# A new instruction order in the second phase of a fused LayerNorm, linear-attention and MLP kernel

## The reference

```python
def reference(x, ...):
    y = layernorm(x)
    h = layernorm(y) * g1 + b1
    q, k, v = h @ wq, h @ wk, h @ wv          # 16 heads of 16
    phi_q, phi_k = elu(q) + 1, elu(k) + 1
    kv, z = sum_s(phi_k * v), sum_s(phi_k)    # per sequence and head
    y2 = y + ((phi_q @ kv) / (phi_q @ z + 1e-6)) @ wo
    h = layernorm(y2) * g2 + b2
    g = table[clip(round((h @ w1) / 0.1))]    # gelu on a grid, 1024 wide
    x = x + y2 + g @ w2
    return x + (layernorm(x) @ CB.T) * (SCB / 127) + bias
```

## Time and profile before

| what | value |
|---|---|
| median of 3 runs | 651.34 us (648.35 to 652.54) |
| time of the profiled execution | 651.4 us |
| its span, first to last instruction | 649.6 us |
| mean granted TensorE clock | 0.975 of full speed |

### The profile page before, as it was taken

One profiled execution on the slowest core, in us unless ns is written; L12 is line 12 of the kernel. 1 busy time (PEld: TensorE's weight loads), 2 busy tenths in 40 slices (PEclk: granted clock), 3 DMA queues, 4 the chain that ended last, 5 costly groups with the idle time before them and its releaser, 6 DMA issues.

```text
span 649.6 us, 12205 instructions
## 1 busy us (share of the span) xinstructions
PE 586.2 (90%) x3838; PEld 517.6 (80%) x3838; DVE 517.0 (80%) x1076; ACT 411.7 (63%) x767; POOL 386.2 (59%) x337
## 2 busy tenths in 40 slices
PE   6999999999997999898998989989899898998875
PEld 6887787878786878788787978879788797887675
DVE  5488988898873688878888788887988878888656
ACT  2377767676765685675756757576665766657560
POOL 3446475655542447676486765757657576675553
PEclk8599999999997999999999999999999999999898
DMA  8101112021101000000100001010110000100001
GB/s 287 53 34 65 59 38 65 32 65 34 66 1 36 17 32 33 32 32 32 65 32 32 33 33 65 32 32 32 32 65 32 32 32 32 65 24 11 33 1 67
DMA packets 11128, 29.16 MB, mean 45 GB/s; under 512 B 2016, under 2 KB 4576, under 8 KB 11104
## 3 DMA queue, kind: packets, MB, share of 16 engines
q1 hardware_dynamic: 9472, 28.32, 12.3%
q10 hardware_dynamic: 1632, 0.53, 0.4%
HBM read 20.45 MB, written 8.39 MB: 44 GB/s over the span
## 4 chain that ended last, share of the span: by engine, by line
PE 36%; DVE 27%; issue 16%; POOL 12%; ACT 6%; DMA 1%; DVEq 1%; ACTq 0%; POOLq 0%; SPq 0%
PE psum L914 31%; DVE f_arena L729 8%; POOL f_arena L355 5%; DVE bn_stats L615 5%; PE psum L932 4%; POOL rstd L324 3%; DVE f_arena L755 3%; DVE f_arena L657 2%; DVE mean_var L622 2%; ACT grid_index L540 2%; DVE f32r_arena L738 2%; POOL pow_arg L322 2%; ACT f32r_arena L550 2%; ACT f32r_arena L494 1%; DVE f_arena L642 1%
## 5 line engine op out<-in xcount | busy, mean ns | idle before, releaser
L914 PE MATMUL psum<-w_hi,f32r_arena 128*128 128x256 f32 x1280 | 178.7, 286 | 5.1 <-DVE f32r_arena L738 3.5
L914 PEld LDWEIGHTS psum<-w_hi,f32r_arena 128*128 128x128 f32 x1280 | 164.9, 190 | 16.0 <-issue 11.5
L914 PE MATMUL psum<-f32r_arena,w_hi 128*128 128x512 f32 x512 | 143.0, 411 | 3.7 <-issue 3.7
L540 ACT ACTIVATE grid_index<-psum,w_bias_in_steps 128x512 int8<-128x512 f32 x128 | 87.2, 681 | 69.9 <-PE psum L914 69.9
L729 DVE TENSOR_SCALAR f_arena<-f_arena,mean_var,rstd 128x256 f32<-128x256 f32 x124 | 102.7, 887 | 25.9 <-POOL rstd L324 25.9
L914 PE MATMUL psum<-f32r_arena 128*128 128x512 f32 (+1 forms) x512 | 120.5, 378 | 2.6 <-issue 1.5
L343 POOL TENSOR_TENSOR f32r_arena<-f_arena,f32r_arena 128x512 fp32r<-128x512 f32 x64 | 86.0, 1344 | 56.3 <-ACT f32r_arena L550 56.3
L914 PEld LDWEIGHTS psum<-f32r_arena,w_hi 128*128 128x128 f32 x512 | 91.1, 194 | 22.4 <-ACT grid_index L540 4.7
L932 PE MATMUL psum<-ident,f_arena 128*128 128x128 f32 x504 | 69.6, 283 | 36.9 <-DVE f_arena L729 32.3
L932 PEld LDWEIGHTS psum<-ident,f_arena 128*128 128x128 f32 x504 | 58.6, 145 | 52.1 <-issue 28.3
L914 PEld LDWEIGHTS psum<-f32r_arena 128*128 128x128 f32 x512 | 83.2, 190 | 14.9 <-issue 3.1
(11 more groups left out here) (96 smaller groups left out, 976.4 us busy)
## 6 DMA issues: line engine op xcount, KB each, us to landing
f_arena<-in_L_attn_x_dram SPq DMA_DIRECT2D x32, 512.0 KB, 3.3
out_dram<-f_arena SPq DMA_DIRECT2D x15, 512.0 KB, 2.6
f_arena<-in_L_attn_w_dram SPq DMA_DIRECT2D x2, 1024.0 KB, 11.3
out_dram<-f_arena SPq DMA_DIRECT2D x2, 256.0 KB, 2.2
phi_q<-in_L_attn_wk_dram ACTq DMA_DIRECT2D x1, 256.0 KB, 4.9
phi_q<-in_L_attn_wv_dram ACTq DMA_DIRECT2D x1, 256.0 KB, 5.4
phi_q<-in_L_attn_wq_dram SPq DMA_DIRECT2D x1, 256.0 KB, 5.7
phi_q<-in_L_ffn_CB_dram SPq DMA_DIRECT2D x1, 256.0 KB, 7.8
```

The source lines that it names most:

```text
L540: act(k8[:, m % 2], bank(AB + m % 2), ACT.Identity, scale=1.0 / STEP, bias=h_bias[:, m:m + 1]).then_inc(s["grid_ready"], 1)
L914: return nc.tensor.matmul(out_, lhs, rhs, start=start, stop=stop, skip_group_check=True)
```

## The change

Phase 2 is put in another order on four engines, and the second norm gets a buffer of its own (`n2t`) instead of sharing `nt`. No operation is added or removed.

```diff
 GpSimd, body
+                if main:
+                    wait(g, s["xp_ready"], i)
+                    g.wait_ge(s["y2_ready"], i + 1)
+                    nc.gpsimd.tensor_tensor(xz, x2[p], y2, ALU.add).then_inc(s["xz_ready"], 1)
                     mlp_low(i, 0)
                 if prv:
                     power(i - 1, u3, r3, mv3, "mv3_ready", "u3_ready", "pow3")
                 if main:
-                    wait(g, s["xp_ready"], i)
-                    g.wait_ge(s["y2_ready"], i + 1)
-                    nc.gpsimd.tensor_tensor(xz, x2[p], y2, ALU.add).then_inc(s["xz_ready"], 1)
                     mlp_low(i, 2)
+                if main:
+                    mlp_low(i, 4)
                 if nxt:
                     power(i + 1, u2, r2, mv2, "mv2_ready", "u2_ready", "pow2")
                 if main:
-                    mlp_low(i, 4)
+                    mlp_low(i, 6)
                 if nn:
                     first_norm(i + 2, p, turn + 1)
-                if main:
-                    mlp_low(i, 6)
 ScalarE, body
                 if main:
-                    quantise(i, 4)
+                    mlp(i, 4)
+                    quantise(i, 5)
                 if prv:
                     a.wait_ge(s["o_done"], o_before_c)
                     high(i - 1, "n3_turned", SA, "s_hi_c")
                 if main:
-                    gelu(i, 4)
-                    mlp(i, 5)
+                    gelu(i, 5)
                     mlp(i, 6)
+                    quantise(i, 7)
                 if nxt:
                     high_h(i + 1)
                 if main:
-                    mlp(i, 7)
+                    gelu(i, 7)
 VectorE, buffers and body
-        take(CE)
+        n2t = take(CE)
...
-            def normalise(c, src, mv, r, powered, done):
+            def normalise(c, src, dst, mv, r, powered, done):
...
-                normalise(c, y2, mv2, r2, "pow2", "n2_ready")
+                normalise(c, y2, n2t, mv2, r2, "pow2", "n2_ready")
...
                 if nxt:
                     first_residual(i + 1)
+                    norm2(i + 1)
                 if prv:
                     low(i - 1, SA, "s_hi_c", "s_lo_c")
-                if nxt:
-                    norm2(i + 1)
+                if main:
+                    mlp_low(i, 5)
                 if prv:
...
                     ve.tensor_tensor(tm(ot), two(SA).rearrange("p (j d) -> p j d", j=TT),
-                if main:
-                    mlp_low(i, 5)
+                if nn:
+                    attend(i + 2, 0)
                 if nxt:
                     low_h(i + 1)
-                if nn:
-                    attend(i + 2, 0)
                 if main:
                     mlp_low(i, 7)
 TensorE, body
                     if main:
                         down(i, 1)
                         up(i, 4)
+                        down(i, 2)
+                        up(i, 5)
                     if prv:
...
                         turn(nt, SA, "n3_turned")
                     if main:
-                        down(i, 2)
-                        up(i, 5)
                         down(i, 3)
                         up(i, 6)
+                        down(i, 4)
                     if prv:
...
                         rows(SA, s_hi, s_lo, cbh, cbl, not exact).then_inc(s["cb_done"], 1)
-                    if nxt and prv:
+                    up(i, 7)
+                    if attend_seq is not None:
+                        attention(i + 2, attend_seq, 0)
+                    if nxt:
                         turn2(i + 1)
-                        up(i, 7)
-                        down(i, 4)
-                        if attend_seq is not None:
-                            attention(i + 2, attend_seq, 0)
                     down(i, 5)
```

More of the change, by code:

```diff
@@ L723, in attend @@
                                      ALU.mult).then_inc(s["attn_tile"], 1)
-            def normalise(c, src, mv, r, powered, done):
+            def normalise(c, src, dst, mv, r, powered, done):
                 v.wait_ge(s[powered], c + 1)
                 for j in range(TT):
-                    i = ve.tensor_scalar(tm(nt)[:, j], tm(src)[:, j], mv[:, 2 * j:2 * j + 1], r[:, j:j + 1],
+                    i = ve.tensor_scalar(tm(dst)[:, j], tm(src)[:, j], mv[:, 2 * j:2 * j + 1], r[:, j:j + 1],
                                          ALU.subtract, ALU.mult)
@@ L789, in body @@
                     v.wait_ge(s["mv3_ready"], i)
-                    normalise(i - 1, xp, mv3, r3, "pow3", "n3_ready")
+                    normalise(i - 1, xp, nt, mv3, r3, "pow3", "n3_ready")
                 if main:
@@ L1096, in turn2 @@
                 pe.wait_ge(s["y2_ready"], c + 1)
-                turn(nt, of_chunk(c, SB2, AB), "n2_turned")
+                turn(n2t, of_chunk(c, SB2, AB), "n2_turned")
             def phase2(exact):
```

## The result

The changed kernel takes 674.26 us (median of 4 runs, 673.53 to 676.41) against 650.99 for the one before in the same comparison: a ratio of 1.037, 95% interval 1.033 to 1.041. It was forecast at 673, slower. The span of the profiled execution is 671.8 us, 22.2 more.

What follows compares the result with a forecast made beforehand. Phase 2's 13 equal bodies were taken as bounding, TensorE near its floor plus waits, with VectorE blocked while GpSimd works. Each body +2.0 us, +26 in all, ends -4.3: 651.4 becomes 673.1 us, range 658 to 690.

Steps and rivals of the forecast that it cites:

- step 1: GpSimd's `xz` ahead of block 0: block 0 and `down(0)` later, cost 0.65 us; first norm done about 10.3, not 12.0.
- T: Clock in us of the predicted walk through one body, starting at that body's `up(0)` on TensorE.
- the 0.65: Predicted cost in us per body of `down(0)` starting later because block 0 queues behind `xz` on GpSimd.
- step 2: n3 turned later on TensorE, behind `down(2)` and `up(5)`: reached at 13.1, norm done, gap of 1.6 us goes.
- step 3: Block 4 ahead of `pow2`, `norm2` ahead of CB's low part: CB starts at 19.0, new gap 2.1, net 0.9 lost.
- step 4: Attention and `turn2` behind `ot`: only `up(7)` covers VectorE's reading of CB; gap 0.5, `turn2` at 23.4.
- step 5: `gelu(7)` behind `high_h` at the body's end: block 7 late, GpSimd's output beside it; `down(7)` at 28.3, gap 1.2.
- the collision: GpSimd's output running beside VectorE's block 7 at the body's end: bounds 0 and 1.4 us, taken as 0.5.
- The sum of a body: Phase 2 body: 24.6 us of work plus gaps 0.2, 0.7, 2.1, 0.5, 1.2 make 29.3, against 27.3.
- The ends: Bodies outside the 13 equal ones: body 0 -0.3 us, body 14 -1.1, body 15 -2.9, together -4.3.
- The falling clock: Rival: granted clock also falls after the new gap at CB, +12 to +22 us, 685 to 695; chance 0.12.
- "It works as drawn": Rival: both TensorE gaps (1.6 + 0.7) go, no wait replaces them: 617 us in whole, 632 in half; chance 0.11.

Runs made afterwards that it cites:

- the two runs on the sum's place: Changed kernel with GpSimd's `xz` between block 0 and the third norm's power: 677.33 us; with `xz` back behind that power: 698.52 us.

## Why the prediction was right

**The sum first (step 1).** Block 0 ran T+4.0 to 5.3 and `down(0)` started at T+5.4, as walked. But the 0.65 can't be taken as a price: with block 0 in time CB started no earlier (T+18.9) and the kernel was slower. The step is right in the walk, and by the two runs on the sum's place the edit was a gain in this order.

**n3 (step 2).** Turned at T+13.0 without a wait (13.1 walked). The norm beside one block took 2.34 us and was done at T+10.0; about 3 us and 10.3 were walked.

**The norm ahead of the low part (step 3).** This is the cause, shown by the run that undoes it alone: 674.3 to 649.5, and 670.1 to 632.3 with GpSimd's output held in both. CB at T+18.8 (19.0 walked), gap 2.0 (2.1). The step's heading names two edits, and one half of it was wrongly accused: block 4 ahead of the power does hold the power, but without it block 4 holds the norm, and with the low part in front it gains 11 us.

**The wait for `ot` (step 4).** Half right. Where the clock stayed full, the attention waited 0.38 for `ot` (0.5 walked); where the clock fell and CB took 2.60 to 3.46, it waited 0 to 0.19. There `up(7)` took 1.33 to 1.91 in place of 1.10, and covered VectorE's reading of CB.

**The end (step 5).** `down(7)` waited 0.81 to 0.94 in bodies with the full clock and 0.47 in the others, walked as 1.2. The 0.5 that I took for the collision in every body was 0.4 in five of thirteen: this is the mis-sized term, and holding the output alone gained 4 us, not 6.5. It grew into the largest loss only in an order that I hadn't thought of.

**The sum of a body.** Walked 29.3, measured 29.05 where the clock stayed up and 29.7 where it fell, 29.45 on the mean. The forecast's body was 0.25 too long, its clock too good: two errors of 3 to 5 us that cancel in part, so the 673.1 against 674.3 is better than the working behind it. That is luck. The split of the sum is off too. By the view, TensorE idled 2.05 us in the body of the earlier trace rows (1.51, 0.47 and small ones), not 2.7, so its work is 25.2, not 24.6; in the changed kernel a body with the full clock has 25.4 of work and waits of 0.38, 1.97, 0.38 and 0.88, together 3.6 and not 4.7. The times of the walk on T don't hang on this split.

**The rivals.** The falling clock was given 0.12 and a price of 12 to 22 us, as another case. It was part of this one: it fell in 8 bodies, and filling the gap took 5 us out of the 13 bodies. I had placed the gap of 2.1 between one that left the clock alone and one that didn't; I should have put a part of the price into the sum. "It works as drawn" was named with the right condition, the low part done before TensorE gets to CB: met by one exchanged pair of lines, and with the collision removed it gave 632 against the 617 to 632 named.

**The ends.** Bodies 14 and 15: -1.5 and -3.2 against -1.1 and -2.9. Body 0 took 0.3 more, not 0.3 less. Together -4.4 against -4.3, which is closer than its parts; the start of phase 2, 1.1 us earlier, belongs to no step.

## What to carry to other kernels

In an order of instructions that wait on each other, ask of each instruction with a wait what stands behind it on its engine and who needs that. A step that is ready belongs ahead of one that waits, when another engine stands for it; the exchange of two such steps was worth 25 us here, and 38 with the collision behind it out of the way. When a gain fails to appear, look at the durations of unchanged instructions: a wait that keeps VectorE and GpSimd apart can be worth more than the time that it costs. And price a place in an order only together with what it hides: moving the sum from ahead of block 0 to behind it cost 3 us in one order and gained 6.5 in another. Last, compare the loop bodies and not the whole time alone, when a part that no edit touches differs by some us from trace to trace.

## What the runs showed of the hardware

VectorE's subtraction of two SBUF tiles (block 7) took 2.83 us in place of 0.69 when GpSimd's sum of 2.34 us started 0.06 us ahead of it. This is the exclusive lock on a port pair that the Trainium skill describes (SBUF — State Buffer, "Who interferes with whom"), here for an instruction with two SBUF inputs, and the trace agrees. What I hadn't expected is how cheaply it is avoided: put one behind the other by a wait, the same two instructions took 0.69 and 2.40 us.

The granted clock went to 1.2 GHz after TensorE's wait of 1.98 us, in 8 of 13 equal bodies, and not in the other five, with the same wait (1.97 in one of them). Before the change it stayed at 2.4 GHz through bodies with gaps of 1.5 and 0.5. The length of the wait alone doesn't tell: the clock fell in 9 bodies of 13 with a wait of 2.8 at CB (sum between block 0 and the power), in all 13 with one of 2.95 (sum behind the power), but only behind 3 of 7 waits of 2.6 ahead of `down(7)` (low part first). What decides between two equal bodies stays open. That the gap is the occasion is shown by the filler: with 1.7 us of useless matmuls in it the clock was 1.00 in every body, and the 13 bodies together 5 us shorter.
